# Two holds for GpSimd's weight splits, and five filler matmuls between layer 0's transposes

## What is computed

```python
x = x + L0_conv(ln(x, eps=1e-6), W_qkv, W_proj, b_proj)   # attention over n, pixel means of q and k
t = x.reshape(-1, 256)
t = t + L0_ffn(ln(t, eps=1e-5), ...)   # softmax gate, top 2 of 8, silu(t @ w1 + b1) @ w2 + b2
x = t.reshape(x.shape)
x = x + L1_conv(ln(x), ...)            # the same form as in layer 0
t = t + L1_ffn(ln(t), ...)             # top 2 of 8, (a * silu(g)) @ W2 + b2, a and g halves of t @ W1 + b1
```

## Time and profile before

| | us |
|---|---|
| median of 3 runs | 591.79 (590.12 to 592.01) |
| the profiled execution: its time | 593.63 |
| its span, first to last instruction | 591.9 |
| PE busy | 544.1 (92%) |
| DVE busy | 338.6 (57%) |
| ACT busy | 333.3 (56%) |
| POOL busy | 280.2 (47%) |
| mean granted PE clock | 0.969 |

### The profile page before, as it was taken

How to read it: one execution, slowest core, us unless ns; L and a number is a source line. 1 busy time by engine, 2 the same in 40 slices (tenths; PEclk the granted TensorE clock), 3 DMA queues, 4 the chain that set the end, 5 groups by cost and what they waited for, 6 DMA issues and landing times.

```text
span 591.9 us, 15435 instructions
## 1 busy us (share of the span) xinstructions
PE 544.1 (92%) x3572; PEld 479.0 (81%) x3573; DVE 338.6 (57%) x719; ACT 333.3 (56%) x605; POOL 280.2 (47%) x331
## 2 busy tenths in 40 slices
PE   7999858999999999999789998699999999999991
PEld 3797525999999989998678874389999999999891
DVE  5448985455544555564884578744655565656330
ACT  3688324566755667665447755254666665666430
POOL 4448214346554466653814260425446555545422
PEclk9799988999999999999999999799999999999996
DMA  7435567455642444235431246532264555322110
GB/s 265 136 107 153 171 210 228 119 150 139 155 83 35 114 123 96 41 88 166 150 100 57 89 144 213 196 120 37 60 193 127 137 137 138 71 76 37 30 27 10
DMA packets 48122, 69.96 MB, mean 118 GB/s; under 512 B 8790, under 2 KB 39648, under 8 KB 48096
## 3 DMA queue, kind: packets, MB, share of 16 engines
q1 hardware_dynamic: 34304, 55.88, 29.4%
q0 software_dynamic: 10464, 13.58, 13.1%
q10 hardware_dynamic: 3328, 0.20, 0.3%
HBM read 57.01 MB, written 13.47 MB: 119 GB/s over the span
## 4 chain that ended last, share of the span: by engine, by line
PE 64%; DMA 13%; DVE 11%; issue 4%; ACT 3%; POOL 3%; POOLq 1%; SPq 0%; DVEq 0%; ACTq 0%
PE banks L1249 14%; PE banks L1251 14%; PE banks L1250 14%; DMA mid_dram<-expert_io,scol 10%; PE banks L1288 5%; PE banks L1457 5%; PE banks L1362 2%; DVE stats L872 2%; PE banks L1426 2%; DVE onehot_row L1095 2%; POOL expert_io L614 2%; PE banks L1257 1%; DVE x_logits L1008 1%; PE banks L1299 1%; DMA xres<-in_x_dram 1%
## 5 line engine op out<-in xcount | busy, mean ns | idle before, releaser
L1249 PE MATMUL banks<-w_hi,xT_hi 128*128 x336 | 119.5, 356 | 4.6 <-DVE xT_lo L1135 2.6
L1249 PE MATMUL banks<-w_hi,hT_hi 128*128 (+2 forms) x392 | 115.8, 295 | 2.0 <-DVE hT_lo L1204 1.3
L1251 PE MATMUL banks<-w_hi,xT_lo 128*128 x336 | 114.9, 342 | 0.0
L1250 PE MATMUL banks<-w_lo,xT_hi 128*128 x336 | 114.3, 340 | 0.0
L1251 PE MATMUL banks<-w_hi,hT_lo 128*128 (+2 forms) x392 | 110.8, 283 | 0.0
L1250 PE MATMUL banks<-w_lo,hT_hi 128*128 (+2 forms) x392 | 110.8, 283 | 0.0
L582 POOL TENSOR_TENSOR w_lo<-raw,w_hi 128x1024 fp32r<-128x1024 f32 (+1 forms) x24 | 62.0, 2604 | 55.8 <-ACT w_hi L663 55.8
L794 ACT COPY banks<-seed_rows 128x1024 f32 (+1 forms) x56 | 64.4, 1151 | 31.0 <-issue 13.5
L1249 PEld LDWEIGHTS banks<-w_hi,hT_hi 128*128 128x128 f32 (+2 forms) x392 | 74.8, 191 | 4.7 <-issue 3.6
L1250 PEld LDWEIGHTS banks<-w_lo,hT_hi 128*128 128x128 f32 (+2 forms) x392 | 75.1, 192 | 0.0
L1251 PEld LDWEIGHTS banks<-w_hi,hT_lo 128*128 128x128 f32 (+2 forms) x392 | 74.9, 191 | 0.0
(11 more groups left out here) (206 smaller groups left out, 899.4 us busy)
## 6 DMA issues: line engine op xcount, KB each, us to landing
raw<-in_L_ffn_w_dram SPq DMA_DIRECT2D x32, 512.0 KB, 4.0
raw<-in_L_ffn_W_dram SPq DMA_DIRECT2D x16, 672.0 KB, 4.1
raw<-in_L_ffn_W_dram SPq DMA_DIRECT2D x16, 336.0 KB, 3.8
seed_rows<-in_L_ffn_b_dram SPq DMA_DIRECT2D x8, 672.0 KB
seed_rows<-in_L_ffn_b_dram SPq DMA_DIRECT2D x8, 512.0 KB
xn_dram<-raw SPq DMA_DIRECT2D x6, 512.0 KB, 3.0
wqkv<-in_L_conv_W_qkv_dram SPq DMA_DIRECT2D x2, 768.0 KB, 5.6
mid_dram<-xres SPq DMA_DIRECT2D x3, 512.0 KB, 4.0
```

The lines of the kernel that those rows point to most:

```text
L1249: pe.matmul(out, hi, w_high, start=first, stop=False, skip_group_check=onto)
L1250: pe.matmul(out, hi, w_low, start=False, stop=False, skip_group_check=onto)
L1251: return pe.matmul(out, lo, w_high, start=False, stop=last, skip_group_check=onto)
```

## The change

It makes four edits. POOL's eleventh split of each layer (`HELD_SPLIT`, index 10) also waits for a new semaphore `x_part`, which DVE raises when L1009 is done. POOL's first split of layer 1 also waits for `last_hot` to reach 4, that is for DVE's second one-hot set. PE gets five fillers in layer 0, behind the transposes of the second pair of tiles. And the four semaphores of the loads of x are shared by the layers, with the count of the second layer doubled, which moves no instruction.

```diff
@@ gpsimd
                 for q in range(PIECES * SLOTS):
                     e, at = q // PIECES, slice((q % PIECES) * w, (q % PIECES + 1) * w)
                     pool.wait_ge(s.first_hi, q + 1)
+                    if q == HELD_SPLIT:
+                        pool.wait_ge(x_part, L + 1)
+                    if L == 1 and q == 0:
+                        pool.wait_ge(last_hot, 4)
                     pool.tensor_tensor(w_lo[:, e, at], raw[:, 0, at], w_hi[:, e, at].bitcast(F32), ALU.subtract
                                        ).then_inc(s.pool_split, 1)
@@ vector
-                    dve.wait_ge((s.x_in0, s.x_in1, s.x_in2, s.x_in2, s.x_in3, s.x_in3)[j], 16)
+                    dve.wait_ge(x_in[(0, 1, 2, 2, 3, 3)[j]], 16 * (L + 1))
@@ vector
-                chain(nc.vector.tensor_tensor(x_logits[:, :, :], x_logits[:, :, :], experts_bc(b_logit[:, :]), ALU.add))
+                nc.vector.tensor_tensor(x_logits[:, :, :], x_logits[:, :, :], experts_bc(b_logit[:, :]), ALU.add
+                                        ).then_inc(x_part, 1)
+                dve.wait_ge(x_part, L + 1)
@@ tensor
                     mm.then_inc(s.xnT_mm, 1)
+                    if L == 0 and j == 1:
+                        keep_busy(BUSY_CHUNK, 6)
```

More of the change, by code:

```diff
@@ L41 @@
 ROW_CHUNKS = 4
-BUSY_LOAD, BUSY_TOP, BUSY_LIST, BUSY_GATHER, BUSY_LAYER, BUSY_LAST = 32, 28, 16, 12, 4, 4
+BUSY_LOAD, BUSY_TOP, BUSY_LIST, BUSY_GATHER, BUSY_LAYER, BUSY_LAST, BUSY_CHUNK = 32, 28, 16, 12, 4, 4, 5
 XT_BANKS = (2, 3, 7, 0, 1, 4)
 EARLY_PAIRS = (1, 2)
+HELD_SPLIT = 10
 SLOTS = 3
@@ L72, in __init__ @@
     def __init__(self, sem, L):
[L73 to L76, removed]
         self.conv_in = sem(f"conv_in_{L}")
@@ L297, in metaformer @@
         rows_added = sem("rows_added")
+        x_in = [sem(f"x_in{i}") for i in range(4)]
+        x_part = sem("x_part")
         last_hot = sem("last_hot")
@@ L405, in load_x @@
                 s = lay[L]
-                for done, a, b in ((s.x_in0, 0, 2), (s.x_in1, 2, 4), (s.x_in2, 4, 8), (s.x_in3, 8, 12)):
+                for done, a, b in zip(x_in, (0, 2, 4, 8), (2, 4, 8, TILES)):
                     sp.dma_start(xres[:, a:b, :], v[:, a:b, :]).then_inc(done, 16)
```

## The result

The changed kernel took **585.65 us** (median of 20 runs, 584.08 to 591.21) against 591.49 us for the kernel before (20 runs, 588.83 to 596.5): ratio 0.9906, 95% interval 0.9885 to 0.9927, so faster by 0.7 to 1.2%. The forecast was 585.3. The profiled execution took 584.60 us, its span 582.8, with a mean granted clock of 0.979.

What follows compares the result with a forecast made beforehand. Three places stood out: DVE stalled behind POOL's splits in layer 0, PE's clock drop at layer 0's start, and the handover. 593.63 - 4.56 - 2.18 + 0.3 = 587.2 us profiled, median 585.3; range 581.4 to 588.0.

Steps and rivals of the forecast that it cites:

- The fillers: PE, start of layer 0: clock holds through the transposes, 2.18 us gained; rival that they don't hold it, 587.5, chance 0.20.
- L884 is held to the end of the fourth split: Layer 1 after the handover: L884 ends 1.7 us late, cutting the gain from 3.6 to 1.9 us.
- The hold of layer 1's eleventh split: Layer 1's projection: L1008 already takes 0.24 us there, so nothing to win; zero.
- the second dip to 7 tenths: Clock row of the earlier profile: a dip in the slice beginning at 296 us, read as the start of layer 1.
- The handover: Hold before layer 1's first split: 1.9 gained, 2.18 lost, net 0.3 us lost; rival that it pays, 583.1 to 581.4, 0.20.
- The hold in layer 0: Layer 0's projection: L1008 ends just behind the tenth split, the last addition comes at 66.96 instead of 71.52; 4.56 us gained.
- the rival of a shorter stall: L1008 in layer 0 usually stalls less: hold saves about 2.2 us (587.7) or nothing (589.9); chance 0.10.
- 2.18 for all: Layer 1, normalisation to k: PE's 3.7 us idle lets the clock fall, 2.18 us lost.
- The sum: Whole kernel: 593.63 - 4.56 - 2.18 + 0.3 = 587.2 us for the profiled execution; median 591.79 - 6.5 = 585.3 us.

Runs made afterwards that it cites:

- the multiplication put ahead of it: The kernel before with two unused DVE instructions, a reduction and a multiplication by 1.0, just ahead of L1008 in layer 0: 590.0 us, one profiled run.
- the best version: The changed kernel plus eight fillers in layer 1, its fourth split held until DVE's first less_mean: 582.81 us, ratio 0.9873 to the kernel before.

## Why the forecast came out

All profiled executions by what was in the kernel, us:

| stretch | without the edit | with it |
|---|---|---|
| normalisation to k, layer 0 (fillers) | 11.08, 11.07, 9.50, 8.90, 8.89, 8.90, 8.89 | 8.89 to 8.90, seven times |
| PE idle ahead of the third transposes, layer 0 (fillers) | 2.33, 2.02, 2.30, 1.63, 1.61, 1.54, 1.07 | 0.1 to 0.92 |
| start of L1008 (or of what was put ahead of it) to first addition, layer 0 (hold of the eleventh split) | 7.14, 7.10, 7.36, 4.60, 4.47, 4.55 | 2.34 to 2.57, seven times |
| k to last addition, layer 0 (the same hold, the same order) | 47.38, 47.37, 47.62, 44.78, 44.78, 44.78 | 42.82 to 42.84, seven times |
| last L1184 to last addition (hold of layer 1's first split) | 17.30, 17.28, 16.13 to 16.14 four times, 22.81 | 15.05 to 15.07, six times |
| normalisation to k, layer 1, held and with no fillers there | 8.89 to 8.90, seven times | 9.50, 9.51, 9.50, 11.36, 11.64 |

**The mechanisms were right.** L1008 is over with the tenth split, at 2.20 us (2.2 forecast). PE's projection sets the last addition, at 11.03 us. The fillers keep the clock. L1184 and L1188 are short in the handover, L884 is held to the end of the fourth split, and PE waits 3.75 us (3.7 forecast) after it, with a fall of the clock each of the five times. The hold of layer 1's eleventh split costs nothing: k to last addition is 42.81 to 42.84 us with and without it.

**One misreading.** The prediction puts the second dip to 7 tenths of the earlier trace rows at 296 us. It is the slice that begins at 369.9 us, 11 us behind the last addition of layer 1, where no edit acts; the slice from 296 us is at 9. The handover's fall of the clock is real, but shorter: the earlier trace rows has 0.83 over 295 to 305 us. No term of the sum hangs on the slice.

**The hold in layer 0, mis-sized.** The 4.56 us were right for the execution that I read (4.54), but a stall of three splits is one of two outcomes. In three of six executions without the hold L1008 (or the multiplication put ahead of it) was passed over by two splits; in three it got in behind the tenth split, and only the bias row lost another. The stage from k to the last addition took 47.4 to 47.6 us in the first three, 44.78 in the others, and 42.83 with the hold. So it is worth 4.5 to 4.8 or 1.95 us, 46.12 - 42.83 = 3.3 on average. The runs agree in the main: 3.1 us alone (0.9947), 1.9 beside the fillers (0.9987 to 0.9955), 3.4 beside the hold in the handover (1.0005 to 0.9947), and from 0.9995 to 0.9906 or 0.9933 with the rest in place, 5.3 or 3.7 us. I had put 0.10 on the rival of a shorter stall, as if it held in all executions or in none; it holds in some.

**The fillers, mis-sized in the same way.** 2.18 us is what the fall of the clock cost in the execution that I read, and I took it as there in every one. It fell in three of seven without fillers, at 2.2, 2.2 and 0.6 us, a mean of 0.7 us, and in none of seven with them. Three of seven against none of seven could be chance; what carries the reading is that the rows of idle time sort all fourteen: it fell after 2.02 to 2.33 us and not after 1.63 or less, and fillers leave at most 0.92. The ratios move by 0.6 to 0.8 us with the fillers, alone (0.9987), beside both holds (0.9947 to 0.9933) and beside the handover's (1.0005 to 0.9995), each within its noise. The price differs too: with the hold in the handover alone the granted clock was back at 1.00 over 19 to 22 us (0.6 us lost), in the kernel before it was still 0.50 there (2.2 us).

The Trainium skill, "TensorE: Matmul & The Clock Gate", Part 4, has transposes not count as PE's activity in the same way. By that rule the fillers couldn't have helped; here the clock stayed full through the transposes behind them all seven times, and through layer 1's after 1.16 to 1.75 us of idle time.

**The handover, mis-sized, its sign open.** Forecast was a loss of 0.3 us net; from the one profiled execution to the other it gained 2.25 - 0.60 = 1.65. Gained are 1.1 us against the usual 16.13, 2.2 where the clock had fallen in the handover without the hold (17.30), and 7.8 where all four splits passed L1184 over (22.81). Given back are 0.6 us in three executions and 2.5 and 2.7 in two, where I had 2.18 for all. Against the usual handover the net is between 0.5 gained and 1.7 lost. The bad executions that the hold removes lift its mean to (17.42 - 15.06) - 1.40 = 1.0 us gained; without the single 22.81 it would be 0.1. The ratios don't settle the sign: 1.0005 for it alone, 0.9987 without it and 0.9995 with it beside the fillers, 0.9947 with and without it beside the hold in layer 0, and 0.9906 or 0.9933 with it against 0.9955 without it beside both. That its cost can be taken back is settled: with fillers in layer 1 and the fourth split held, the stretch and the stage behind it are 13.05 + 8.90 us, where the change has 15.05 + 9.50.

**The sum.** The means are 3.3 + 0.7 + 1.0 = 5.0 us; measured were 5.6 (0.9906) and 4.0 (0.9933). The forecast of 6.5 added 4.56 and 2.18 and took off 0.3, so two terms too large by 2.7 us met one too small by 1.3. That 585.3 lies so near to 585.65 is luck in part: errors of the terms cancel, and the median of the kernel before alone differs by up to 1.85 us between the groups (591.49 and 589.64). The profiled execution came out 2.6 us below its forecast of 587.2, by 1.3 from the start and 0.6 from the end, 1.9 from the handover, less 1.2 in the expert loop.

**The scatter.** The single runs of the kernel before have a standard deviation of 1.7 to 2.1 us, those of the change 1.7 and 1.1, of the hold in layer 0 alone 1.3, of the fillers alone 2.2, of the best version 1.0 (six runs). The first 20 runs of the change hardly differ in that from the 20 beside them (1.9), so a narrower scatter isn't shown for it. Of the 169 runs of kernels without the hold in the handover seven took 595.6 us or more, of the 81 with it none. One handover of 22.81 us, in an execution of 594.45 us, is what such runs would look like, but none of the seven was profiled.

**Open.** What decides whether DVE gets in between two splits: the same program did and didn't. So the 4.55 us with one split queued may be that count or chance. The expert loop of layer 0 took 215.93 to 218.27 us over all kernels, whatever the edit. In the 35 us behind layer 0's last addition the granted clock was 0.90 in all seven kernels with the full hold in layer 0, and 0.85 in five of the seven without it; the prediction has no term for that, and the expert loop's mean shows no gain by it. In the changed kernel's profile PE waited 1.36 us there for a gather, while 2 MB of expert weights were on their way; whether that load delayed the gather was not tried.

## What to carry to other kernels

Where two engines contend for one resource and one of them has a queue of long instructions, hold back the queue just behind the point where the other must pass, as long as nobody waits for the held work; ask then what the held work meets later, since a hold moves a collision (here to L884) as well as removing one. A time that is 28 times what the same instruction takes elsewhere (6.80 against 0.24 us) may be one outcome of several: profile several executions before pricing its removal. Here the hold in layer 0 alone brought 3.1 us, near the mean of its outcomes (3.3) and not the one that was read (4.56). An engine made to run ahead can end in an idle time, as PE's 3.75 us here; if its clock falls there, fillers should go in with the speed-up.

## What the hardware showed

- A DVE instruction that meets back-to-back POOL instructions isn't always served when the one in flight ends. It was passed over by two more (6.80 us), by three more (9.46 us), or by none (2.10 to 2.23 us for L1008, 2.17 to 2.19 us for L1184). The Trainium skill, "SBUF — State Buffer", "Who interferes with whom", has the one that issues first hold the shared ports for its whole instruction; by that rule it would wait for no more than one split, which the trace goes beyond.
- Who is stalled, by rows beside running splits: products, sums and `scalar_tensor_tensor` with two operands in SBUF, and the multiplication of one operand by a constant (6.45 us). Not stalled: the reduction of the same tile (0.25 us, one execution) and additions with an operand in PSUM (0.69 us). The same section of the skill lists `tensor_scalar` among the operations that can take both ports and `tensor_reduce` among those that never contend on trn2; the trace agrees with both.
- PE's clock, by stretches: after 2.02, 2.30 and 2.33 us of idle time at the transposes of layer 0 it went towards its lower level (1.2 GHz; 0.52 over 15 to 22 us in the earlier trace rows), after 1.07 to 1.63 us it stayed at 2.4 GHz. After 3.75 to 3.77 us in layer 1 it fell in five of five, at a price between 0.6 and 2.7 us, after 1.16 to 1.75 us in none of eight.
